# Squares summed in four column tiles, the root moved ahead, and low parts of the first scan's weights moved between normalisation and rotation

## The chip, the cores and the metric

One core of a Trainium2 chip runs the whole program. The time is device microseconds of one execution. A kernel is run several times and the median is given.

## The reference, cut to what matters

A block of three parts runs over `x`, four sequences of 512 tokens with 256 features: half a mixture of experts, a state-space layer with 64 heads, and the same mixture again. Both changed pieces sit in the middle part:

```python
Bm = (x @ WB.T).reshape(B_, L, H, N)          # H = 64 heads, N = 128
Cm = (x @ WC.T).reshape(B_, L, H, N)
Bm = rmsnorm(Bm, Bn_w) + B_bias               # x * rsqrt(mean(x*x) + EPS) * w
Cm = rmsnorm(Cm, Cn_w) + C_bias
theta_cumsum = jnp.cumsum(theta * dt[..., None], axis=1)
Bm = rope(Bm, theta_cumsum)                   # rotation of pairs of features
Cm = rope(Cm, theta_cumsum)
h = at * h + bt * B_prev x_prev + gt * Bt xt  # scan over the tokens of a sequence
yt = einsum('bhn,bhnp->bhp', Ct, h)
```

## The kernel before, in words

**Stages.** A first mixture of experts, then four scans (one for each sequence, numbered 0 to 3), then the second mixture. A short routing stage lies between scans 1 and 2. Scans 0 and 1 also gather rows of the first mixture's result (`gather_turn_pool`, `gather_turn_dve`, L803 on DVE), and scans 2 and 3 scatter rows for the second one.

**A scan.** 64 heads are 32 pairs (`n` counts them through all scans, `q` in one scan). After a preparation (`prep_pe` and the like) the pairs go through a software pipeline. `turn_pe`, `turn_act`, `turn_pool`, `turn_dve` and `turn_sp` each write out a body of four pairs, `j` = 0 to 3, that a hardware loop repeats. The order on each engine is what stands in these functions. Nothing else schedules. In what follows a *turn* is the part of one pair `n`, an *odd* turn one with odd `j`, and a *step* (period) the time from one turn to the next. Engines run freely and wait for each other's semaphores: `e_...` are counted by engines, `a_...` by DMAs.

**What a turn does on each engine**, in this order:

- PE: `ss_pe(n+2)` sums squares (below). `Y_pe(n-2)` (L1391, L1393) makes outputs and waits for DVE's `K_dve2` of the turn before. `G_pe(n-1)` (L1327) multiplies rotated B by rotated C. `tr_pe` (L1336) transposes B. `A_pe(n+3)` (L63, `wb`) projects B and C with a high and a low part of the weights, halves [0, 1] and [2, 3], with `K2_pe` (L1367) between them. `T_pe(n+2)` (L63, `th`) projects the angles.
- ACT: `T_act3` makes cosine and sine, `T_act2` (L1162) rounds the running sum of the angles, `R_act` (L1213, odd turns, needs another function table) takes the root, `K_act` (L1342) copies the transposes out of PSUM, which frees the bank that `A_pe` writes next, and `A_act` (L1206, L1208) copies the projections out and squares them.
- DVE: `T_dve1` (L1148, L1151, waits for `T_pe`), `F_dve2` (L1257, L1262), `T_dve2` (L1157, waits for `T_act2`), `K_dve1` (L1351, waits for `G_pe`), `Y_dve` (odd turns), `F_dve1` (L1251 twice, the normalisation), `R_dve` (L1218, odd turns, the reciprocal of the root), `F_dve3` (L1275 four times, the rotation's products), the gather's L803 in scans 0 and 1, and `K_dve2` (L1376, the states).
- POOL: `D_pool` (L1300), `own_pool` (L1295, waits for `F_dve1`), `F_pool` (L1283, L1284 twice, completes the rotation, waits for `F_dve3`).
- SP issues the DMAs.

**Sums of squares.** `ss_pe` multiplies the squares (`sq4`, [128, 4, 512]: even and odd features of B and of C) by a matrix of ones and zeros. It is four matmuls with 32 result rows each into one PSUM bank: B's in partitions 0 to 31, C's in 32 to 63 (a column tile of PE each), even and odd features added up. The fp32 matmul has two records in the trace. Two turns fill the bank. In the odd turn `R_act` takes the root of 36 rows of 512, `R_sp1` moves eight of them into `rc_in` [128, 32], `R_dve` inverts, `R_sp2` writes them to DRAM and `R_sp3` reads them back copied over all partitions (`rr_bc`), for `F_dve1` of the next turns.

**Scan 0's weights.** Projections use weights split in a high part (fp32 rounded by a copy) and a low part (the difference). Scan 0 makes both and stores them in DRAM (`watt_dram`). Later scans only load them. For each pair in scan 0: SP loads the raw weights (`wb_load_sp` L1023 into `keep`, `th_load_sp` L1031 into `th_raw`), ACT copies (`wb_high_act` L1053, `th_high_act` L1067), DVE subtracts (`wb_low_dve` L1057, `th_low_dve` L1071, both operands in SBUF), and SP stores (L1038, L1043). Raw weights have one buffer, so a load waits for the low part of the pair before, and the high part waits for the load. In the kernel before, the two low parts stand behind rotation and gather:

```python
                F_dve3(e, n, j, q, [1])
                if gathers(b):
                    gather_turn_dve(e, b, n, q, it, j)
                if is_first(b) and not last:
                    wb_low_dve(e, q + 4, j)
                if is_first(b) and not (last and j >= 1):
                    th_low_dve(e, q + 3, j + 1)
                if K:
                    K_dve2(e, p, jp, b * NB + it + (j > 0))
```

## Time and profile before

| | |
|---|---|
| median of 3 runs | 3599.38 us (3589.8 to 3600.61) |
| the profiled execution | 3601.3 us, its span 3599.5 us |
| busy in the span | PE 2897.9 us, DVE 2374.4 us, ACT 1820.9 us, POOL 1539.4 us |
| mean granted clock of TensorE | 0.882 of full speed |
| sums of squares, L1197 | 1024 records, 246.0 us busy |
| low parts, L1057 and L1071 | 32 of each, most of them 2.3 and 1.5 us |
| scans' steady parts, from the span's start | scan 0 700 to 1190 us, scan 1 1360 to 1770, scan 2 1990 to 2400, scan 3 2560 to 2970 |

Busy time is the union of an engine's instructions. Ends of matmuls are modelled, so neighbours overlap by some tenths of a us. Both mixtures and the routing between are not touched by the change. The granted clock is a share of 2.4 GHz.

### The profile page before, as it was taken

What the parts mean: (1) busy time and instruction counts of PE and PEld (TensorE: products, weight loads), DVE (VectorE), ACT (ScalarE), POOL (GpSimd) and SP (SyncE); (2) the same over time, 40 slices, a digit from 0 to 9 for tenths busy, and PEclk for the clock granted to TensorE, in tenths of its full rate; (3) what the DMA queues carried; (4) which work ended last, traced back from release to release, by engine and by line L of the source; (5) the groups of instructions that cost most, each with busy time, mean ns of one, the idle gap of its engine ahead of it and who ended that gap; (6) DMA issues with size and microseconds to landing.
All of it is one profiled execution on the core that took longest, in us unless ns stands there. A gap on an engine that the chain in (4) does not pass through costs nothing.

```text
span 3599.5 us, 84310 instructions
## 1 busy us (share of the span) xinstructions
PE 2897.9 (81%) x28752; PEld 2199.6 (61%) x28752; DVE 2374.4 (66%) x3926; ACT 1820.9 (51%) x3740; POOL 1539.4 (43%) x1420
## 2 busy tenths in 40 slices
PE   5139957788888899999977999999899998279573
PEld 4128846466666657667654667676676676168462
DVE  5214224699999849889945988884888885243135
ACT  1016624566666356666614666663666672046331
POOL 3550050255555416655610555551455553510345
PEclk7559968889899899999978999998999998589785
DMA  9537755466665246556403666642666653467564
GB/s 387 197 123 254 255 163 179 142 183 184 177 184 176 77 139 171 164 162 171 134 3 119 173 172 172 171 134 68 170 172 171 172 160 115 158 206 254 175 205 138
DMA packets 311258, 605.54 MB, mean 168 GB/s; under 512 B 59136, under 2 KB 159616, under 8 KB 310016
## 3 DMA queue, kind: packets, MB, share of 16 engines
q1 hardware_dynamic: 286464, 535.63, 48.9%
q0 software_dynamic: 24576, 67.14, 5.6%
q8 instruction: 120, 1.97, 0.2%
q14 instruction: 98, 0.80, 0.1%
HBM read 446.25 MB, written 155.32 MB: 167 GB/s over the span
## 4 chain that ended last, share of the span: by engine, by line
PE 53%; DVE 19%; issue 10%; another core or an unknown queue 7%; ACT 4%; DMA 4%; POOL 1%; DVEq 1%; SPq 1%; POOLq 0%; ACTq 0%
PE bank L63 15%; PE bank L568 7%; PE bank L1327 4%; DVE tmp L1275 3%; PE bank L1197 3%; PE bank L1393 3%; DVE xbc L1251 3%; DMA rc_in<-decay_t 3%; PE bank L581 2%; PE bank L559 2%; PE bank L1391 2%; PE cs_sn L581 2%; PE bank L1367 2%; DVE rot L1275 2%
## 5 line engine op out<-in xcount | busy, mean ns | idle before, releaser
L63 PE MATMUL bank<-xh,wb 128*128 128x512 f32 x2048 | 685.4, 416 | 73.1 <-ACT btr L1342 43.2
L644 DVE TENSOR_TENSOR hh<-sg,bank 128x96 f32<-128x96 f32 x384 | 97.5, 254 | 596.4 <-ACT sg L619 372.6
L63 PEld LDWEIGHTS bank<-xh,wb 128*128 128x128 f32 x2048 | 373.3, 192 | 190.4 <-ACT btr L1342 63.9
L1206 ACT ACTIVATE xbc<-bank,norm_w 128x512 f32<-128x512 f32 x512 | 350.7, 685 | 240.8 <-PE bank L63 234.1
L1295 POOL TENSOR_TENSOR sq<-cst,rho 128x512 f32<-128x512 f32 x128 | 133.5, 1043 | 742.8 <-DVE xbc L1251 411.3
L1283 POOL TENSOR_TENSOR rot<-rot,tmp 128x512 f32<-128x512 f32 x256 | 341.8, 1335 | 238.3 <-DVE tmp L1275 238.3
L568 PE MATMUL bank<-wgu,xgT 128*128 (+1 forms) x1536 | 343.7, 350 | 107.6 <-issue 68.2
L63 PE MATMUL bank<-xl,wb 128*128 128x512 f32 x1024 | 408.5, 399 | 0.0
L1284 POOL TENSOR_TENSOR rot<-rot,tmp 128x512 f32<-128x512 f32 x256 | 358.7, 1401 | 0.0
L568 PEld LDWEIGHTS bank<-wgu,xgT 128*128 128x128 f32 x1536 | 261.0, 204 | 118.5 <-issue 118.1
L1275 DVE SCALAR_TENSOR_TENSOR rot<-xbc,bias,cs_sn 128x1024 f32<-128x1024 f32 x256 | 325.4, 1271 | 8.4 <-DVE xbc L1251 6.8
L1275 DVE SCALAR_TENSOR_TENSOR tmp<-xbc,bias,cs_sn 128x1024 f32<-128x1024 f32 x256 | 326.2, 1274 | 0.0
L1251 DVE TENSOR_TENSOR xbc<-xbc,rr_bc 128x1024 f32<-128x1024 f32 x256 | 311.7, 1258 | 1.9
L1208 ACT ACTIVATE sq<-bank 128x512 f32<-128x512 f32 x512 | 303.7, 593 | 5.0 <-PE bank L1197 5.0
L1197 PE MATMUL bank<-sq,cst 128*32 128x512 f32 x1024 | 246.0, 601 | 21.7 <-ACT sq L1208 21.7
L1342 ACT ACTIVATE btr<-bank 128x512 f32<-128x512 f32 x256 | 142.0, 594 | 235.4 <-PE bank L1336 235.2
L1393 PE MATMUL bank<-st,rot 128*64 128x16 f32 x3584 | 252.4, 217 | 0.0
L1391 PEld LDWEIGHTS bank<-x1p,sq 128*64 128x64 f32 x2048 | 139.2, 146 | 182.0 <-issue 135.1
L1393 PEld LDWEIGHTS bank<-st,rot 128*64 128x64 f32 x3584 | 239.8, 149 | 0.0
L63 PEld LDWEIGHTS bank<-xl,wb 128*128 128x128 f32 x1024 | 195.9, 191 | 48.6
L574 PE MATMUL cs_sn<-ident,hh 128*96 128x128 f32 x384 | 111.0, 289 | 139.5 <-issue 104.4
L1391 PE MATMUL bank<-x1p,sq 128*64 128x16 f32 x2048 | 150.7, 216 | 80.4 <-DVE st L1376 80.1
(277 smaller groups left out, 6084.7 us busy)
## 6 DMA issues: line engine op xcount, KB each, us to landing
wb<-watt_dram SPq DMA_DIRECT2D x96, 1024.0 KB, 7.7
rr_bc<-rr_dram SPq DMA_DIRECT2D x128, 512.0 KB
yd<-ys SPq DMA_DIRECT2D x96, 512.0 KB
wd<-w_down SPq DMA_DIRECT2D x384, 96.0 KB
watt_dram<-wb SPq DMA_DIRECT2D x32, 1024.0 KB, 5.4
dt_bc<-row_dram SPq DMA_DIRECT2D x256, 128.0 KB
al_bc<-row_dram SPq DMA_DIRECT2D x256, 128.0 KB, 3.2
xd<-xg SPq DMA_DIRECT2D x12, 2048.0 KB, 23.7
```

What stands on the lines that cost most here:

```text
L63: ins = e.matmul(dst, a, m, start=start and c == 0, stop=stop and c == n - 1, skip_group_check=not (start and stop))
L568: ins = e.matmul(gub[n % 2][:, 0:NI2], xgT[n % 2][:, k, :], w, start=k == 0, stop=k == KD - 1)
L581: e.matmul(dnb[n % 2][:, 0:D], hT[n % 2][:, :], wd[n % NWD][:, :], start=True, stop=True).then_inc(e_dn.sem, 1)
L1197: ins = e.matmul(SSB[32 * ty:32 * ty + 32, :], one_hot[:, first:first + 32], sq4[:, 2 * ty + eo, :], start=j % 2 == 0 and eo == 0, stop=j ...
L1206: e.activation(xbc[j % 4][:, i, :], of(i)[:, :], ACT.Copy, scale=norm_w[:, i:i + 1])
L1208: e.activation(sq4[:, i, :], of(i)[:, :], ACT.Square).then_inc(e_X.sem, 1)
L1251: e.tensor_tensor(both, both, r.unsqueeze(1).to_broadcast([P, 2, SEQ]), ALU.mult).then_inc(dst.sem, 1)
L1275: ins = e.scalar_tensor_tensor(o[:, 2 * ty:2 * ty + 2, :], X[:, i, :].unsqueeze(1).to_broadcast([P, 2, SEQ]), bias_of(i), cs_sn[:, :, :], ...
L1283: e.tensor_tensor(R[:, 2 * ty, :], R[:, 2 * ty, :], tmp[:, 2 * ty + 1, :], ALU.subtract)
L1284: ins = e.tensor_tensor(R[:, 2 * ty + 1, :], R[:, 2 * ty + 1, :], tmp[:, 2 * ty, :], ALU.add)
L1391: e.matmul(o, m1[:, (a * TT + t) * CL:(a * TT + t + 1) * CL], c4(x1p[j][:, :])[:, a * TT + t], start=True, stop=True)
L1393: ins = e.matmul(y[CL:P, k, w:w + PW].rearrange("p (a d) -> p a d", a=2), R[:, 2 + eo, CL * k:CL * k + CL], hist[:, eo, :, :, k], start=eo ...
```

## The change

Four things change, the first three in all scans, the last in scan 0 alone.

1. `ss_pe` works on halves of 256 tokens: eight matmuls instead of four, each of 256 columns instead of 512, at partitions 0, 32, 64 and 96 (four column tiles). The result lies in 100 rows of 256. `R_act` takes the root of that, into a buffer of its own (`stdr`, [100, 256]) instead of rows of `decay_t`. `R_sp1` and `R_sp2` each issue two DMAs instead of one.
2. On ACT, `R_act` stands ahead of `T_act2` instead of behind it.
3. On SP, `R_sp1` stands ahead of the transfers of `dt_bc`, `end_bc`, `th` and `wb` instead of behind them.
4. In scan 0, DVE's low parts stand between normalisation (with `R_dve`) and rotation. The angle weights' parts are made in the turn that uses them instead of the turn before. ACT's high parts stand ahead of `K_act` instead of near the end of the turn. SP loads raw angle weights at the end of its turn.

```diff
--- before.py
+++ after.py
@@ -184,8 +184,9 @@
         neg_a = sb("neg_a", [NH, 1])
         bias = sb("bias", [P, NP, 4])
         norm_w = sb("norm_w", [P, 4])
-        stdr = decay_t[0:36, :, :, :].rearrange("p k q a -> p (k q a)")
-        NORM_ROWS = slice(28, 36)
+        HALF = SEQ // 2
+        stdr = sb("stdr", [100, HALF])[:, :]
+        NORM_ROWS = [slice(28, 36), slice(92, 100)]
         rc_in, rc = sb("rc_in", [P, 32]), sb("rc", [P, 32])
 
         dks = [xc[:, i, :] for i in range(2)]
@@ -1192,10 +1193,12 @@
                 e.wait_ge(e_sr.sem, e_sr.at(m // 2 if isinstance(m, int) else m >> 1))
             e.wait_ge(e_X.sem, e_X.at(4 * (m + 1)))
             for eo in range(2):
-                for ty in range(2):
-                    first = 30 - 28 * (1 - ty) - 2 * (j % 2)
-                    ins = e.matmul(SSB[32 * ty:32 * ty + 32, :], one_hot[:, first:first + 32], sq4[:, 2 * ty + eo, :],
-                                   start=j % 2 == 0 and eo == 0, stop=j % 2 == 1 and eo == 1, skip_group_check=True)
+                for half in range(2):
+                    for ty in range(2):
+                        first = 30 - 28 * (1 - ty) - 2 * (j % 2)
+                        g = 64 * half + 32 * ty
+                        ins = e.matmul(SSB[g:g + 32, 0:HALF], one_hot[:, first:first + 32], sq4[:, 2 * ty + eo, half * HALF:(half + 1) * HALF],
+                                       start=j % 2 == 0 and eo == 0, stop=j % 2 == 1 and eo == 1, skip_group_check=True)
             ins.then_inc(e_ssm.sem, 1)
 
         def A_act(e, m, j, parts=range(4), of=by_turns):
@@ -1209,12 +1212,12 @@
 
         def R_act(e, gm):
             e.wait_ge(e_ssm.sem, e_ssm.at(2 * (gm + 1)))
-            e.wait_ge(a_r1.sem, a_r1.at(gm))
-            e.activation(stdr, SSB[0:36, :], ACT.Sqrt, scale=1.0 / NS, bias=eps_nm[0:36, 0:1]).then_inc(e_sr.sem, 1)
+            e.wait_ge(a_r1.sem, a_r1.at(2 * gm))
+            e.activation(stdr, SSB[0:100, 0:HALF], ACT.Sqrt, scale=1.0 / NS, bias=eps_nm[0:100, 0:1]).then_inc(e_sr.sem, 1)
 
         def R_dve(e, gm):
-            e.wait_ge(a_r1.sem, a_r1.at(gm + 1))
-            e.wait_ge(a_r2.sem, a_r2.at(gm))
+            e.wait_ge(a_r1.sem, a_r1.at(2 * (gm + 1)))
+            e.wait_ge(a_r2.sem, a_r2.at(2 * gm))
             e.reciprocal(rc[:, :], rc_in[:, :]).then_inc(e_rc.sem, 1)
 
         e_rc = ev("e_rc")
@@ -1224,15 +1227,18 @@
             e.nop(nofuse=True)
             e.wait_ge(e_rc.sem, e_rc.at(gm))
             e.nop(nofuse=True)
-            e.dma_start(rc_in[:, :], stdr[NORM_ROWS, :].rearrange("r (c w) -> r c w", w=32)).then_inc(a_r1.sem, 16)
+            for h in range(2):
+                e.dma_start(rc_in[CL * h:CL * h + CL, :], stdr[NORM_ROWS[h], :].rearrange("r (c w) -> r c w", w=32)).then_inc(a_r1.sem, 16)
 
         def R_sp2(e, gm, par):
             e.wait_ge(e_rc.sem, e_rc.at(gm + 1))
             e.nop(nofuse=True)
-            e.dma_start(rr_dram[par].rearrange("r (c w) -> (r c) w", w=32), rc[:, :]).then_inc(a_r2.sem, 16)
+            for h in range(2):
+                dst = rr_dram[par][:, h * HALF:(h + 1) * HALF].rearrange("r (c w) -> r c w", w=32)
+                e.dma_start(dst, rc[CL * h:CL * h + CL, :]).then_inc(a_r2.sem, 16)
 
         def R_sp3(e, gm, par):
-            e.wait_ge(a_r2.sem, a_r2.at(gm + 1))
+            e.wait_ge(a_r2.sem, a_r2.at(2 * (gm + 1)))
             e.nop(nofuse=True)
             e.wait_ge(e_xcc.sem, e_xcc.at(2 * (gm - 1)))
             e.nop(nofuse=True)
@@ -1467,10 +1473,14 @@
                     stage_act(e, b, n, q, it, j)
                 if not (first and j == 0):
                     T_act3(e, n, j)
+                if RG:
+                    R_act(e, gm + 1)
                 if T:
                     T_act2(e, n + 1, j + 1)
-                if RG:
-                    R_act(e, gm + 1)
+                if is_first(b) and not last:
+                    wb_high_act(e, q + 4, j, it * 2 + j // 2 + 2)
+                if is_first(b) and not (last and j >= 2):
+                    th_high_act(e, q + 2, j, it * 2 + j // 2 + 1)
                 if K:
                     K_act(e, p, jp, 0, 0)
                 if last and j >= 2:
@@ -1485,10 +1495,6 @@
                     A_act(e, n + 3, j + 3, [1], behind_transposes)
                 if RG:
                     e.activation(std[:, 0:1], half_pi[:, 0:1], ACT.Sin)
-                if is_first(b) and not last:
-                    wb_high_act(e, q + 4, j, it * 2 + j // 2 + 2)
-                if is_first(b) and not (last and j >= 1):
-                    th_high_act(e, q + 3, j + 1, it * 2 + (j + 1) // 2 + 1)
                 if A:
                     A_act(e, n + 3, j + 3, [2, 3], behind_transposes)
 
@@ -1530,14 +1536,14 @@
                 F_dve1(e, n, j, b * NB + it + 1)
                 if RG:
                     R_dve(e, gm + 1)
+                if is_first(b) and not last:
+                    wb_low_dve(e, q + 4, j)
+                if is_first(b) and not (last and j >= 2):
+                    th_low_dve(e, q + 2, j)
                 F_dve3(e, n, j, q, [0])
                 F_dve3(e, n, j, q, [1])
                 if gathers(b):
                     gather_turn_dve(e, b, n, q, it, j)
-                if is_first(b) and not last:
-                    wb_low_dve(e, q + 4, j)
-                if is_first(b) and not (last and j >= 1):
-                    th_low_dve(e, q + 3, j + 1)
                 if K:
                     K_dve2(e, p, jp, b * NB + it + (j > 0))
 
@@ -1552,8 +1558,10 @@
                     wb_store_sp(e, q + 3, j + 1)
                 if is_first(b) and not last:
                     wb_load_sp(e, b, q + 4, j)
-                if is_first(b) and not (last and j >= 2):
-                    th_store_sp(e, q + 2, j)
+                if is_first(b) and not (first and j == 0) and not (last and j == 3):
+                    th_store_sp(e, q + 1, j + 1)
+                if RG:
+                    R_sp1(e, gm + 1)
                 if not (last and j >= 2):
                     e.wait_ge(e_tu.sem, e_tu.at(n + 1))
                     e.nop(nofuse=True)
@@ -1561,7 +1569,7 @@
                     e.wait_ge(e_H.sem, e_H.at(n - 1))
                     e.nop(nofuse=True)
                     end_sp(e, q + 2, j + 2)
-                if not (last and j >= 1):
+                if not is_first(b) and not (last and j >= 1):
                     e.wait_ge(e_th.sem, e_th.at(n + 2))
                     e.nop(nofuse=True)
                     th_load_sp(e, b, q + 3, j + 1)
@@ -1570,8 +1578,6 @@
                     e.nop(nofuse=True)
                     if not is_first(b):
                         wb_load_sp(e, b, q + 4, j)
-                if RG:
-                    R_sp1(e, gm + 1)
                 if not (last and j >= 2):
                     e.wait_ge(e_D.sem, e_D.at(n + 1))
                     e.nop(nofuse=True)
@@ -1579,6 +1585,8 @@
                 if RG:
                     R_sp2(e, gm + 1, (j // 2 + 1) % 2)
                     R_sp3(e, gm + 1, (j // 2 + 1) % 2)
+                if is_first(b) and not (last and j >= 1):
+                    th_load_sp(e, b, q + 3, j + 1)
 
         def pairs_pe(e, b):
             N, NB, G = b * NP, NP // UN, b * (NP // 2)
@@ -1606,7 +1614,6 @@
             A_act(e, N + 2, 2, [0, 1])
             T_act3(e, N, 0)
             if is_first(b):
-                th_high_act(e, 2, 0, 1)
                 wb_high_act(e, 3, 1, 1)
             A_act(e, N + 2, 2, [2, 3])
             e.wait_ge(e_x12.sem, e_x12.at(b + 1))
@@ -1637,8 +1644,6 @@
             N, NB, G = b * NP, NP // UN, b * (NP // 2)
             T_dve1(e, N, 0, G + 1)
             T_dve2(e, N, 0)
-            if is_first(b):
-                th_low_dve(e, 2, 0)
             if is_first(b):
                 wb_low_dve(e, 3, 1)
             turn_dve(e, b, 0, True, False)
```

In the lists below, line numbers are those of each kernel: most of the changed kernel's are 1 to 10 higher. First DVE, an odd turn of scan 0, before:

```order
L1251 TENSOR_TENSOR xbc<-xbc,rr_bc 128x1024 x2
L1218 RECIPROCAL rc<-rc_in 128x32
L1275 SCALAR_TENSOR_TENSOR rot<-xbc,bias,cs_sn 128x1024
L1275 SCALAR_TENSOR_TENSOR tmp<-xbc,bias,cs_sn 128x1024
L1275 SCALAR_TENSOR_TENSOR rot<-xbc,bias,cs_sn 128x1024
L1275 SCALAR_TENSOR_TENSOR tmp<-xbc,bias,cs_sn 128x1024
L803 SCALAR_TENSOR_TENSOR keep<-ykq,w,keep 128x256
L1057 TENSOR_TENSOR wb<-keep,wb 128x1024
L1071 TENSOR_TENSOR th<-th_raw,th 128x256
L1376 SCALAR_TENSOR_TENSOR st<-end_bc,bank 64x128 x2
```

and the same turn in the changed kernel:

```order
L1257 TENSOR_TENSOR xbc<-xbc,rr_bc 128x1024 x2
L1221 RECIPROCAL rc<-rc_in 128x32
L1058 TENSOR_TENSOR wb<-keep,wb 128x1024
L1072 TENSOR_TENSOR th<-th_raw,th 128x256
L1281 SCALAR_TENSOR_TENSOR rot<-xbc,bias,cs_sn 128x1024
L1281 SCALAR_TENSOR_TENSOR tmp<-xbc,bias,cs_sn 128x1024
L1281 SCALAR_TENSOR_TENSOR rot<-xbc,bias,cs_sn 128x1024
L1281 SCALAR_TENSOR_TENSOR tmp<-xbc,bias,cs_sn 128x1024
L804 SCALAR_TENSOR_TENSOR keep<-ykq,w,keep 128x256
L1382 SCALAR_TENSOR_TENSOR st<-end_bc,bank 64x128 x2
```

The two low parts moved from behind the gather to behind the reciprocal.

ACT, the start of an odd turn of scan 0, before (the high parts came near the turn's end):

```order
L1170 ACTIVATE cs_sn<-ths,half_pi 128x512
L1162 ACTIVATE bank<-cum,magic 128x512
L1213 ACT_TABLE_LOAD
L1213 ACTIVATE decay_t<-bank,eps_nm 36x512
L1342 ACTIVATE btr<-bank 128x512 x2
...
L1487 ACT_TABLE_LOAD
L1487 ACTIVATE std<-half_pi 128x1
L1053 ACTIVATE wb<-keep 128x1024
L1067 ACTIVATE th<-th_raw 128x256
```

and now:

```order
L1171 ACTIVATE cs_sn<-ths,half_pi 128x512
L1216 ACT_TABLE_LOAD
L1216 ACTIVATE stdr<-bank,eps_nm 100x256
L1163 ACTIVATE bank<-cum,magic 128x512
L1054 ACTIVATE wb<-keep 128x1024
L1068 ACTIVATE th<-th_raw 128x256
L1348 ACTIVATE btr<-bank 128x512 x2
```

Root and table load are ahead of the rounding, and the high parts are ahead of the copies of the transposes.

SP, an odd turn of scan 0 in the changed kernel, from its second DMA on:

```order
L1024 DMA keep<-w_att 128x1024
L1044 DMA watt_dram<-th 256x1x256
L1231 DMA rc_in<-stdr 64x1x32 x2
L1127 DMA dt_bc<-row_dram 64x512 x2
L1127 DMA end_bc<-row_dram 64x128 x2
L1127 DMA al_bc<-row_dram 64x512 x2
L1238 DMA rr_dram<-rc 8x8x32 x2
L1247 DMA rr_bc<-rr_dram 64x4x512 x2
L1032 DMA th_raw<-w_att 128x256
```

`rc_in` was one DMA between `end_bc` and `al_bc`, and `th_raw` stood ahead of it. Now `th_raw` is the last of the turn, behind `rr_bc`.

## Rows read from the trace of the kernel before

**Rows 1.** Busy time by stage, scans 0, 1, 2: PE, PEld, DVE, ACT, POOL; clock, DMA share, GB/s.

```profile
700.00:1190.00 490.00, 429.51 (x5068) 322.16 (x5069) 473.23 (x545) 310.20 (x550) 267.20 (x218) 0.91 0.62 181
1360.00:1770.00 410.00, 388.97 (x4960) 286.68 (x4960) 366.42 (x476) 268.41 (x476) 239.11 (x211) 0.99 0.58 165
1990.00:2400.00 410.00, 390.79 (x5064) 287.33 (x5063) 364.31 (x464) 284.21 (x518) 237.89 (x219) 1.00 0.60 170
```

**Rows 2.** Line L1218, once in two turns: ns min/median/max, first to last start (scans 0 to 2).

```profile
L1218 DVE RECIPROCAL rc<-rc_in x14: 345/348/353, 705.8 to 1171.2; 128x32 f32<-128x32 f32 x14
L1218 DVE RECIPROCAL rc<-rc_in x13: 345/352/354, 1379.8 to 1753.1; 128x32 f32<-128x32 f32 x13
L1218 DVE RECIPROCAL rc<-rc_in x14: 343/352/354, 1991.4 to 2382.3; 128x32 f32<-128x32 f32 x14
```

**Rows 3.** Waits, 1360 to 1770 us (scan 1): us in total, times, longest.

```profile
DVE sq L1351 <- PE bank L1327: 15.7, 26, 1.0
DVE bank L1148 <- PE bank L63: 10.8, 12, 2.1
DVE rc L1218 <- DMA rc_in<-decay_t: 8.9, 9, 1.2
```

**Rows 4.** Waits, 1990 to 2400 us (scan 2).

```profile
DVE sq L1351 <- PE bank L1327: 14.1, 27, 1.0
PE bank L63 <- ACT btr L1342: 13.0, 27, 1.1
DVE rc L1218 <- DMA rc_in<-decay_t: 12.7, 12, 1.8
DVE bank L1148 <- PE bank L63: 10.7, 13, 1.2
```

**Rows 5.** Timeline, one `ss_pe` of scan 2: start, us, engine, instructions merged.

```profile
2206.43 1.91 PE L1197 MATMUL bank<-sq,cst 128*32 128x512 f32 x8
2206.43 0.14 PEld L1197 LDWEIGHTS bank<-sq,cst 128*32 128x32 f32 x4 [0.37 <-ACT sq L1208]
2206.89 0.12 PEld L1197 LDWEIGHTS bank<-sq,cst 128*32 128x32 f32 x2 [0.31 <-issue]
2207.32 0.12 PEld L1197 LDWEIGHTS bank<-sq,cst 128*32 128x32 f32 x2 [0.31 <-issue]
```

**Rows 6.** Timeline of scan 0: DVE around the low parts, and POOL there.

```profile
961.12 2.29 DVE L1057 TENSOR_TENSOR wb<-keep,wb 128x1024 fp32r<-128x1024 f32 x1
963.32 1.48 DVE L1071 TENSOR_TENSOR th<-th_raw,th 128x256 fp32r<-128x256 f32 x1
964.73 0.84 DVE L1376 TENSOR_TENSOR_SCAN st<-end_bc,bank 64x128 f32<-64x128 f32 x2
...
960.85 1.47 POOL L1283 TENSOR_TENSOR rot<-rot,tmp 128x512 f32<-128x512 f32 x1
962.28 2.25 POOL L1284 TENSOR_TENSOR rot<-rot,tmp 128x512 f32<-128x512 f32 x1
...
973.25 1.04 POOL L1295 TENSOR_TENSOR sq<-cst,rho 128x512 f32<-128x512 f32 x1 [2.69 <-DVE xbc L1251]
```

**Rows 7.** Lines L1057 and L1071, all of scan 0, ns min/median/max.

```profile
L1057 DVE TENSOR_TENSOR wb<-keep,wb x32: 1215/2295/2317, 613.1 to 1176.8; 128x1024 fp32r<-128x1024 f32 x32
L1071 DVE TENSOR_TENSOR th<-th_raw,th x32: 418/1485/1503, 614.3 to 1193.7; 128x256 fp32r<-128x256 f32 x32
```

**Rows 8.** Timeline of scan 0: SP's issue of a raw load, ACT's rounding and high part; then DMA's median us to landing.

```profile
946.09 0.41 SPq L1023 DMA_DIRECT2D keep<-w_att  x1
...
949.20 0.69 ACT L1162 ACTIVATE bank<-cum,magic 128x512 f32<-128x512 f32 x1 [3.71 <-DVE cum L1151]
...
958.62 1.05 ACT L1053 ACTIVATE wb<-keep 128x1024 fp32r<-128x1024 f32 x1
...
keep<-w_att SPq DMA_DIRECT2D x32, 512.0 KB, 6.0
```

**Rows 9.** Timeline of scan 2's preparation on ACT: the root behind `ss_pe`.

```profile
1951.90 1.28 ACT L1213 ACT_TABLE_LOAD   x1 [3.54 <-PE bank L1197]
```

## The prediction

> **What bounds the kernel now.** The page's busy times name PE (81% of the span), but a share of the whole says little here, so I first read busy time stage by stage. In scan 0 DVE is busy 473 of 490 us and PE 430 [rows 1]: DVE is the bound. In scans 1 and 2 PE is busy 389 and 391 of 410 us, DVE 366 and 364: PE is the bound and DVE follows closely. The change touches the four scans only.
>
> The next view is the start of one instruction that comes once in two turns, L1218 [rows 2]. It gives the step per turn: scan 0 (1171.2 - 705.8) / 13 / 2 = 17.9 us, scan 1 (1753.1 - 1379.8) / 12 / 2 = 15.55, scan 2 (2382.3 - 1991.4) / 13 / 2 = 15.03. Scan 3 runs the same body as scan 2, and I take scan 2's step for it.
>
> The third view is the waits. They tell what stands second in line, which decides how much of a saving is kept. In scan 1 (410 / 15.55 = 26.4 turns) DVE waits 15.7 us for `G_pe`, 10.8 for `T_pe` and 8.9 for `rc_in`: 1.34 us a turn [rows 3]. Without any wait DVE would need 15.55 - 1.34 = 14.2 us a turn. In scan 2 (27.3 turns) the same three are 14.1, 10.7 and 12.7 us, 1.37 a turn, so DVE's floor is 13.66 [rows 4]. PE waits there 13.0 us, 0.48 a turn, for ACT's copy of the transposes.
>
> **Squares in four column tiles.** One `ss_pe` takes 1.91 us [rows 5]. Its eight records do not run one after another: four weight loads start at 2206.43 (for the first two slots), two at 2206.89 and two at 2207.32. So a slot is 0.44 us and holds two records. Four slots of 0.44 and an end of 0.15 give 1.91. The two column tiles already run side by side, with different moving data. The changed form has 16 records of half the columns. If four run side by side, there are again four slots, each of 0.22: 4 x 0.22 + 0.15 = 1.03 us. That saves **0.88 us a turn**. Four loads must fit into a slot: at the start four loads take 0.14 us together [rows 5], less than 0.22.
>
> No row shows four column tiles of 32 at once, so the bounds are: no gain (two at a time, eight slots of 0.22) and 0.88. I take 0.88, since the pair in the rows loses nothing against its own slots.
>
> The rows show the loads of 2206.89 inside the 1.91 us, beside a running pair. The Trainium skill ("TensorE: Matmul & The Clock Gate", Part 3) says that weight loads overlap running matmuls only where the row group differs, which column tiles of full height never do: by that rule loads stand outside the slots (rival d), and the trace does not agree with it for two tiles. For three column tiles the same page states a speedup of 2.38, not 3; by that, an estimate of the saving would be 0.65 us a turn.
>
> In scans 2 and 3 PE is the bound, so the step falls from 15.03 to about 14.15. DVE's floor is 13.66, and a part of the waits behind it stays, since DVE and PE hand work to each other twice in a turn. I take 14.2, a saving of 0.85. Not all 32 turns run steadily; I count 30 a scan. 60 x 0.85 = **51 us**. In scan 1 the step falls from 15.55 to 14.67, above DVE's floor of 14.2, and I take the same 0.85: 30 x 0.85 = **25 us**. The bounds of this term: below, half of it, if DVE's alternation of short and long turns becomes the bound; above, DVE's floors themselves, 1.37 x 60 + 1.34 x 30 = 122 us instead of 76. In scan 0 PE is not the bound, and this part is worth nothing.
>
> **The root first, on ACT and on SP.** In odd turns `R_act` starts before the rounding. It removes no work. DVE's wait for `rc_in` (0.47 us a turn in scan 2 [rows 4]) goes, but DVE waits in these scans only because PE is late, so by itself this gives nothing; it pays by lowering the floor that part one runs into, and is counted there. The price is on the same engine. The table load starts only when `ss_pe` is done [rows 9], takes 1.28 us, and the rounding now stands behind it, with `T_dve2` behind that. In the best case this is hidden (`ss_pe` ends before the turn's `T_act3` does) and costs nothing; in the worst the whole load shows, 1.28 us in each odd turn, 0.64 a turn. DVE's floor in scans 2 and 3 would then be 13.66 + 0.64 = 14.3 instead of the 14.2 I take, 6 us in 60 turns. I take nothing, since a shorter `ss_pe` also ends earlier. The two extra DMA issues at `R_sp1` and `R_sp2` add about 1 us to SP in odd turns, and its transfers of `dt`, `end`, `th` and `wb` wait for the root. They are for the next turn or later, 14 us away; I cost them at nothing.
>
> **Low parts in scan 0.** Alone, in the preparation, the two take 1.215 and 0.418 us. Inside a turn almost all take 2.3 and 1.49 [rows 7]. The timeline says why [rows 6]. The first starts at 961.12 while POOL's L1283 runs until 962.32, and ends 1.1 us after that, at 963.41. POOL's L1284 starts at 962.28, takes 2.25 us, and ends 1.1 us after the low part did. The second low part starts at 963.32 and ends 0.27 us after POOL's 964.53. So one engine at a time has what both need. From 961.12 to 964.73 DVE spends 3.61 us on work that takes about 1.14 + 0.34 = 1.48 us alone.
>
> In the new place POOL has one instruction, L1295, 1.04 us [rows 6], which starts when the normalisation ends, just when the low parts do. Whichever goes first, DVE passes it once: 1.48 + 0.96 = 2.44 us. The saving is 3.61 - 2.44 = **1.17 us a turn**, 30 x 1.17 = **35 us**. Bounds: 0 if POOL's work meets DVE elsewhere instead, and 2.13 a turn, 64 us, if L1295 gets out of the way.
>
> The same rule is in the Trainium skill ("SBUF — State Buffer", on the port pair shared by VectorE and GpSimd): two SBUF inputs on VectorE against a GpSimd read block each other fully. The trace agrees, as far as [rows 6] show. By that rule the rotation's products, which read one operand from PSUM, do not meet POOL at all, and the bound of 0 would drop out.
>
> What lies beside: PE in scan 0 needs 429.5 / 490 x 17.9 = 15.7 us a turn, less 0.88, so 14.8 against the new step of 16.7 [rows 1]. The high part's copy (1.05 us for `wb` [rows 8], a fourth of the columns for `th`) now stands in front of ACT's `K_act` and delays `A_pe` by up to 1.4 us. PE's 1.9 us of slack covers it, and costs it if gone. The raw load must also come sooner. Now it is issued at 946.09, lands 6.0 us later at 952.1, and is used at 958.62. In the changed order it is needed right behind the rounding, which ends at 949.89, less the 1.2 us by which the turn gets shorter: 948.7 [rows 8]. But it also starts sooner, since the low part it waits for has four products (L1275) and the gather behind it instead of ahead, some 5 us: 941 + 6.0 = 947. About 1.7 us are left.
>
> **The sum.** 51 + 25 + 35 = 111 us against the profiled execution's own 3601.3 us: 3490. The median of the runs lies 1.9 us below that execution. I predict **3488 us**.
>
> **Rivals.**
>
> (a) *Two tiles at a time.* The new form gives eight slots of half the length, no gain; only scan 0 gains. 3601 - 35 = 3566 us. For it: no row shows four. Against it: nothing in the rows makes two special. Chance 0.10.
>
> (b) *Scan 0 gains nothing.* The raw load is late, ACT waits for it in front of `K_act`, and PE behind ACT. If it lands 5 us later than above, 1.7 and PE's remaining slack are used up and the 1.17 us go too: 3488 + 35 = 3523 us. Scans 1 to 3 are as forecast. Chance 0.10.
>
> (c) *Slower.* The 16 records run one at a time, because a load and a matmul of another tile shut each other out. `ss_pe` would take 16 x 0.22 + 0.15 = 3.7 us, 1.8 more. In scans 1 to 3 that is 90 x 1.8 = 162 us on the bound; in scan 0 PE would need 17.5 us, more than the 16.7, so 35 shrinks to 12. 3601 - 12 + 162 = 3751 us. It decides from the point where the records start less than 1.6 at a time: then the loss passes scan 0's 35 us. The pairs in [rows 5] speak against it. Chance 0.03.
>
> (d) *Loads outside the slots.* Four tiles run together, but each slot first waits for its four loads, 0.14 us [rows 5]: 0.56 a turn of the 0.88 is lost, 0.32 stays. 3601 - 90 x 0.32 - 35 = 3537 us. For it: a slot of 0.22 leaves loads half the time they had. Chance 0.05.
>
> **How the numbers follow.** My forecast has 0.72, with its own range of 3455 (DVE near its floors) to 3525 (half of PE's saving, scan 0 as taken). To leave out no more than 2 in 10, the range goes from 3455 to 3545; it holds (b) and (d) and leaves out (a), (c) and some 0.05 of worse mixtures. About 0.3%, 11 us, is what a measurement of this kernel can tell from no change. Faster than that: all but (c) and worse mixtures, 0.95. Within: 0.02. Slower: (c) and a little, 0.03.
>
> **What would show it.** The 16 records of a `ss_pe` in about 1.0 us, loads four at a time (right), in 1.9 (a) or over 3 (c). Steps per turn from the reciprocal's starts: 16.7, 14.7, 14.2, 14.2. DVE busy 95% or more in scans 2 and 3, and no wait for `rc_in`. In scan 0 low parts that take 2.2 + 0.3 or 1.2 + 1.3 us, and POOL's L1284 at 1.3 us throughout. Wrong: ACT waiting for the raw load, DVE's `T_dve2` waiting for ACT's rounding, or a lower granted clock in scans 1 to 3 than 0.99.

## The result, and the profile after

The changed kernel takes 3693.69 us (median of 4 runs, 3682.48 to 3701.94) against 3594.59 for the kernel before, a ratio of 1.027 (95% interval 1.024 to 1.031). The forecast was 3488 us and faster. The profiled execution of the changed kernel took 3687.81 us.

Busy time by stage, a stretch of scans 0, 1 and 2 each (columns as in [rows 1]):

```profile
740.00:1170.00 430.00, 361.66 (x4504) 287.58 (x4504) 371.97 (x465) 261.21 (x465) 224.05 (x187) 0.84 0.58 177
1385.00:1780.00 395.00, 352.34 (x4671) 278.72 (x4671) 333.74 (x439) 243.45 (x434) 219.67 (x194) 0.93 0.55 158
2050.00:2430.00 380.00, 336.86 (x4624) 265.83 (x4626) 315.80 (x403) 246.84 (x454) 206.05 (x192) 0.94 0.55 162
```

PE is busy 89% in scans 1 and 2, where it was 95% [rows 1], and its granted clock is 0.93 and 0.94 where it was 0.99 and 1.00: part of each scan runs at 1.2 GHz. DVE is busy less in scan 0, as meant. No engine is nearer to full than before, so something between the engines must be late. The starts of the reciprocal, once in two turns, are to be set beside [rows 2]:

```profile
L1221 DVE RECIPROCAL rc<-rc_in x14: 343/345/347, 703.4 to 1180.9; 128x32 f32<-128x32 f32 x14
L1221 DVE RECIPROCAL rc<-rc_in x12: 343/343/346, 1389.5 to 1750.0; 128x32 f32<-128x32 f32 x12
L1221 DVE RECIPROCAL rc<-rc_in x12: 339/346/347, 2019.2 to 2371.3; 128x32 f32<-128x32 f32 x12
```

The steps are 18.4, 16.4 and 16.0 us a turn, where the forecast had 16.7, 14.7 and 14.2 and the kernel before has 17.9, 15.6 and 15.0. Scan 3 is slower too (16.2 against 15.1).

The two local effects came as forecast. One `ss_pe` of scan 2 (timeline, as [rows 5]), and the low parts of scan 0 with POOL beside them (as [rows 6]):

```profile
2200.70 1.07 PE L1200 MATMUL bank<-sq,cst 128*32 128x256 f32 x16
2200.70 0.59 PEld L1200 LDWEIGHTS bank<-sq,cst 128*32 128x32 f32 x16 [0.37 <-ACT sq L1211]
...
962.12 1.16 DVE L1058 TENSOR_TENSOR wb<-keep,wb 128x1024 fp32r<-128x1024 f32 x1
963.20 1.26 DVE L1072 TENSOR_TENSOR th<-th_raw,th 128x256 fp32r<-128x256 f32 x1
964.38 1.27 DVE L1281 SCALAR_TENSOR_TENSOR rot<-xbc,bias,cs_sn 128x1024 f32<-128x1024 f32 x1
...
962.24 1.94 POOL L1301 TENSOR_TENSOR sq<-cst,rho 128x512 f32<-128x512 f32 x1 [4.00 <-DVE xbc L1257]
```

The squares take 1.07 us instead of 1.91, with all sixteen loads inside them: four column tiles run together. From the first low part to the rotation DVE spends 964.38 - 962.12 = 2.26 us instead of 3.61. L1301 takes 1.94 us here and 1.04 in [rows 6]: it ends 0.9 us after the first low part, so the two pass one after the other. The Trainium skill ("SBUF — State Buffer", "Who interferes with whom") says that a VectorE instruction with two SBUF inputs contends with a GpSimd instruction that reads SBUF. The trace agrees, by the same 1.94 us against 1.04.

The loss is in the waits. Those of scan 2 (1990 to 2400 us, beside [rows 4]):

```profile
DVE xbc L1257 <- DMA rr_bc<-rr_dram: 42.1, 12, 5.6
PE bank L1397 <- DVE st L1382: 24.7, 12, 4.5
...
SPq L1227 <- ACT stdr L1216: 133.4, 13, 11.8
SPq L1242 <- DMA rr_dram<-rc: 47.3, 12, 4.4
```

DVE's normalisation waits for the broadcast of the reciprocals, a wait that [rows 4] don't have. SP issues its transfers in the order of the program. It stands 133 us at `R_sp1` for the root, and then 3.9 us each time for the small write of the reciprocals to land. The chain of waits from SP's hold-up to DVE (start, us, what):

```profile
2236.41 0.70 SPq L1231
...
2241.15 0.60 SPq L1034
...
2242.09 0.58 SPq L1026
...
2244.19 1.44 SPq L1238
...
2245.68 4.76 DMA rr_dram<-rc
...
2250.65 0.64 SPq L1247
...
2251.33 7.42 DMA rr_bc<-rr_dram
...
2259.92 1.23 DVE xbc L1257
```

Read it downwards. The root's transfer, then `dt`, `end`, `th` (L1034) and the 1 MB of `wb` (L1026) all go out in one burst, since they stood behind the root. The small write (L1238) is issued 2.1 us after the `wb` load and takes 4.8 us to land; only then may its broadcast go, 7.4 us more.

In scan 0 the waits (700 to 1200 us) are others:

```profile
ACT wb L1054 <- DMA keep<-w_att: 61.9, 13, 7.9
PE bank L63 <- ACT btr L1348: 47.2, 27, 6.0
DVE bank L1149 <- PE bank L63: 32.9, 13, 3.7
```

ACT waits for the raw load in front of its copies of the transposes, PE waits for the copies, DVE for PE.

### The profile page after: what moved, and what is told of

It is laid out like the page before. It is cut to its first block, busy times and chain, and to the rows that moved or that the text cites. A ratio compares the mean times of both kernels' runs of the same rounds, so it can differ in the third digit from the quotient of the medians.

```text
span 3686.0 us, 86397 instructions
## 1 busy us (share of the span) xinstructions
PE 2877.2 (78%) x29776; PEld 2280.2 (62%) x29776; DVE 2327.2 (63%) x3926; ACT 1810.0 (49%) x3740; POOL 1531.5 (42%) x1420
## 4 chain that ended last, share of the span: by engine, by line
PE 33%; DMA 17%; issue 13%; DVE 12%; SPq 11%; ACT 6%; another core or an unknown queue 6%; POOL 2%; DVEq 0%; ACTq 0%; POOLq 0%
DMA rr_bc<-rr_dram 7%; PE bank L569 7%; PE bank L63 7%; DMA rr_dram<-rc 5%; SPq L1127 4%; DMA keep<-w_att 3%; DVE tmp L1281 3%; PE bank L560 2%; PE cs_sn L582 2%; DVE xbc L1257 2%; PE bank L582 2%; SPq L1231 2%; DVE rot L1281 1%; PE bank L1333 1%
## 5 line engine op out<-in xcount | busy, mean ns | idle before, releaser
L63 PE MATMUL bank<-xh,wb 128*128 128x512 f32 x2048 | 706.0, 427 | 113.6 <-ACT btr L1348 77.9
L63 PEld LDWEIGHTS bank<-xh,wb 128*128 128x128 f32 x2048 | 386.7, 199 | 231.6 <-ACT btr L1348 97.6
L1301 POOL TENSOR_TENSOR sq<-cst,rho 128x512 f32<-128x512 f32 x128 | 151.2, 1181 | 876.3 <-DVE xbc L1257 556.1
L1289 POOL TENSOR_TENSOR rot<-rot,tmp 128x512 f32<-128x512 f32 x256 | 340.7, 1331 | 246.3 <-DVE tmp L1281 246.3
L63 PE MATMUL bank<-xl,wb 128*128 128x512 f32 x1024 | 417.8, 408 | 0.0
L1257 DVE TENSOR_TENSOR xbc<-xbc,rr_bc 128x1024 f32<-128x1024 f32 x256 | 307.7, 1243 | 147.9 <-DMA rr_bc<-rr_dram 146.0
L1290 POOL TENSOR_TENSOR rot<-rot,tmp 128x512 f32<-128x512 f32 x256 | 330.2, 1290 | 0.0
L1397 PE MATMUL bank<-x1p,sq 128*64 128x16 f32 x2048 | 159.5, 221 | 156.4 <-DVE st L1382 156.0
L1397 PEld LDWEIGHTS bank<-x1p,sq 128*64 128x64 f32 x2048 | 147.6, 154 | 211.7 <-DVE st L1382 122.9
L1399 PE MATMUL bank<-st,rot 128*64 128x16 f32 x3584 | 272.0, 223 | 3.7 <-issue 3.7
L1399 PEld LDWEIGHTS bank<-st,rot 128*64 128x64 f32 x3584 | 259.0, 158 | 3.8 <-issue 3.8
L1333 PE MATMUL bank<-rot 64*64 64x64 f32 x8192 | 208.0, 259 | 30.3 <-POOL rot L1290 20.8
```

Source lines behind the costliest of these rows:

```text
L63: ins = e.matmul(dst, a, m, start=start and c == 0, stop=stop and c == n - 1, skip_group_check=not (start and stop))
L1257: e.tensor_tensor(both, both, r.unsqueeze(1).to_broadcast([P, 2, SEQ]), ALU.mult).then_inc(dst.sem, 1)
L1289: e.tensor_tensor(R[:, 2 * ty, :], R[:, 2 * ty, :], tmp[:, 2 * ty + 1, :], ALU.subtract)
L1290: ins = e.tensor_tensor(R[:, 2 * ty + 1, :], R[:, 2 * ty + 1, :], tmp[:, 2 * ty, :], ALU.add)
L1301: e.tensor_tensor(blocks(own), constant("diag_mask").unsqueeze(1).to_broadcast([P, 2 * TT, CL]), r.unsqueeze(2).to_broadcast([P, 2 * TT, C ...
L1333: ins = e.matmul(o, R[h, eo, CL * k:CL * k + CL], R[h, 2 + eo, CL * k:CL * k + CL], start=eo == 0, stop=eo == 1)
```

## Experiments

The kernel before takes 3595 to 3599 us in some series of runs (that of the result, and two experiments below) and 3344 to 3354 us in the others. These are called the *first chip* and the *second chip* below. The names stand for the two levels of time: the record has several chip numbers for the second, and one of them (8) for both. About 231 of the 250 us lie before the first reciprocal of scan 0 and behind the fifteenth of scan 3. The steps are nearly the same: 17.9, 15.2, 15.0, 14.9 on the second, 17.9, 15.6, 15.1, 15.1 on the first. Ratios are always to the kernel before in the same series. A step is the mean over 24 turns, from the third to the fifteenth reciprocal of a scan. All ran on the second chip unless said otherwise.

A step from one profile has its own scatter. The fastest version below, profiled twice, has 14.8 and 15.1 us in scan 2. Differences in a step under 0.3 us are no evidence.

**The kernel before on the second chip.**

> The kernel before, for its profile on the chip of the experiments, where its median was 3349 us. Theory one (the square kernel's freed TensorE time turns into idle time and then into stretches at the lower of the clock's two levels): in scan 2 this profile shows the granted clock at 1.00, no L1327 or L1336 group of a turn that takes 2 us, and a step per turn of 15.1 to 15.2 us, the same as with the squares in four tiles (15.13). Theory two (this chip itself has such stretches, whatever the kernel): the clock is 0.93 to 0.97 here too, and the steps of the squares' kernel can be compared with these as they stand.

Measured: 3349.9 us (one run), clock 0.915, steps as above; clock 1.00 in scans 1 and 2 and 0.99 in scan 3. This is theory one. In its SP timeline the write follows the `wb` load by 8.6 us, and SP waits for it 11.9 us in 11 turns (1990 to 2400 us):

```profile
2102.95 0.57 SPq L1025 DMA_DIRECT2D wb<-watt_dram  x1
2105.31 0.71 SPq L1227 DMA_DIRECT2D rc_in<-decay_t  x1
2111.59 0.32 SPq L1232 DMA_DIRECT2D rr_dram<-rc  x1
2113.19 1.29 SPq L1241 DMA_DIRECT2D rr_bc<-rr_dram  x2
...
SPq L1236 <- DMA rr_dram<-rc: 11.9, 11, 2.0
```

**The changed kernel with root's transfers put back.**

```
 turn_sp:  -  if RG: R_sp1(...)      (ahead of the wait for e_tu)
           +  if RG: R_sp1(...)      (behind the wb load, ahead of the wait for e_D)
```

> The changed kernel with R_sp1 back behind the loads of dt, end, th and wb on SP (all scans); all else as changed. Theory A (order on SP: the root's issue holds the 1 MB load of wb back until just ahead of the small write of rc, which then waits behind it in the queue): steps of scans 1 to 3 fall from about 16.1 to 14.2 to 14.6 us, the write of rc lands within 2 us, DVE's wait for rr_bc goes, total 3510 to 3550 us; scan 0 stays near 18.4 us a turn. Theory B (the doubled small DMAs, more issues and more packets' latency): DVE still waits for rr_bc, total over 3640 us.

Measured: 1.000 (0.998 to 1.003); steps 18.3, 15.4, 14.7, 14.9. DVE's wait for `rr_bc` is gone (0.9 us from 1850 to 2450 us). The changed kernel has 1.025 to 1.027 on the first chip, and this one has 1.000 on the second, so the slowdown goes with this one line. The comparison crosses the chips, since the changed kernel was not run on the second. The next experiment stays on the second chip. Theory A is right on the wait and wrong on the time: the forecast gain does not come.

**Only root's transfers first,** the kernel before with `R_sp1` ahead of the wait for `e_tu`:

> The kernel before with R_sp1 moved ahead of dt, end, th and wb on SP and nothing else. Theory A: the write of rc lands after 4 to 5 us instead of 1.5, DVE waits for rr_bc, steps of scans 1 to 3 rise by 0.5 to 1.3 us: total 3640 to 3720 us. Theory B: there is no doubled DMA, so no difference, 3595 us.

Measured: 1.049 (1.046 to 1.051), and in a second series, again on the second chip, 1.050 (1.047 to 1.052); steps 17.8, 17.2, 16.9, 16.9. It is theory A's mechanism, at more than its price (0.5 to 1.3 us a turn expected, about 1.9 measured). Scan 0, which has no `wb` load from `watt_dram`, loses nothing. The write's time to landing from 1850 to 2450 us, for the kernel before (there on this chip) and then for this one, with this one's chain of waits in scan 2:

```profile
DMA to landing us min/median/max: 1.4/1.4/3.8
```

```profile
DMA to landing us min/median/max: 2.3/6.0/7.7
...
2053.62 0.56 SPq L1025
...
2055.70 5.32 DMA rr_dram<-rc
2061.21 0.63 SPq L1241
2061.89 6.77 DMA rr_bc<-rr_dram
...
2077.66 1.23 DVE cum L1151
...
2079.62 1.28 ACT L1213
2080.92 0.69 ACT decay_t L1213
2081.72 0.69 SPq L1227
```

It is a closed loop: broadcast, DVE down to the next prefix sum, root, SP's burst, write, broadcast. Two turns take 33.7 us on average.

**Is it the `wb` load that holds the write?** The changed kernel, in odd turns of scans 1 to 3 with that load behind `R_sp3`:

```
 -  if not is_first(b): wb_load_sp(e, b, q + 4, j)
 +  if not is_first(b) and not RG: wb_load_sp(e, b, q + 4, j)
 ...
    R_sp3(...)
 +  if RG and not last and not is_first(b): wb_load_sp(e, b, q + 4, j)
```

> The changed kernel with the root's transfers still first, but in odd turns of scans 1 to 3 the 1 MB load of wb moved behind R_sp3. Theory A: the small write of rc no longer stands behind 1 MB, lands in 1.5 to 2.5 us instead of 4.7, and the wait for rr_bc falls from 3.5 us in two turns to under 1: total 3520 to 3570 us, unless wb itself comes late (then PE waits for it and the step is over 15). Theory B: no change, 3690 us.

Measured: 1.073 (1.071 to 1.076). Steps of scans 1 to 3: 17.7, 17.7, 17.5. SP's wait for the write fell to that of the kernel before, and PE now waits for the load itself (1990 to 2400 us):

```profile
SPq L1242 <- DMA rr_dram<-rc: 11.9, 11, 1.3
...
PE bank L63 <- DMA wb<-watt_dram: 69.2, 12, 7.6
```

So the load does hold the write, and it has no 5 us to give: "for the next turn or later" was wrong for it too. DVE's wait for `rr_bc` falls from 146.0 us in the whole execution to 65.8 and does not go, though the write lands quickly. What is left may be the length of SP's burst itself; no run separates it.

**The root early on both engines,** and **the changed kernel again** (on the first chip):

> e4 with the root ahead of the rounding on ScalarE as well, squares and scan 0 as before. Steps of scans 1 to 3 so far: 15.2 to 15.0 before, 17.2 to 16.9 with the transfers first, 16.4 to 16.0 in the changed kernel. Theory one (the early root lets SP go on sooner, and that is why the changed kernel pays only half): steps 15.9 to 16.4, the wait for rr_bc 130 to 160 us in place of 206, ratio 1.022 to 1.035. Theory two (the squares, which bring the sum 0.84 us sooner, are the other half): steps 16.5 to 16.8, ratio over 1.035.

> The changed kernel itself on the chip of the experiments, to have its parts and their sum beside one another: squares alone 1.005, root's transfers first alone 1.049, all but the transfers 1.000. Theory one (transfers first is what makes it slower, and its cost is about that of e4 less what the other parts give): 1.035 to 1.055. Theory two (on the first chip it was 1.027, and the earlier root on ScalarE gives back part of the cost, since SP is held up for less time): 1.020 to 1.035.

Measured: 1.021 (1.019 to 1.024), steps 17.9, 15.9, 15.8, 15.9, wait for `rr_bc` 147.5 us; and 1.025 (1.022 to 1.028), steps 18.1, 16.4, 16.0, 16.0, wait 136.6 us. The first is theory one, with steps and ratio at the lower edge of its ranges. The second falls in theory two's range, but on the first chip. The early root frees SP sooner: its wait for the root falls from 656.3 us in the whole execution (transfers first alone) to 493.6, and the price from 4.9% to 2.1%, both on the second chip. SP's wait for the write to land is nearly the same in both (232.8 and 223.8 us). So the held write is one part of the loop's length, and the time at which the root comes is another. The squares are not needed for the lower price: without them it is no higher.

**Only the squares.** The kernel before with four column tiles and the transfers that they need:

> The kernel before with the squares in four column tiles and the doubled DMAs alone; orders on ACT and SP and scan 0's low parts as before. Theory A: each ss_pe 1.07 instead of 1.91 us, steps of scans 1 to 3 near 14.7, 14.3, 14.3, scan 0 17.9: total 3520 to 3545 us. Theory B: DVE waits longer for rc_in (one more issue of 0.7 us) or for rr_bc, total 3580 us or more.

Measured: 1.005 (1.003 to 1.007); steps 18.3, 15.5, 15.1, 15.1; clock 0.888. Theory A's gain is not there, and DVE's wait for `rc_in` is longer, as in theory B (76.9 us against 64.2). Stages of 24 turns in scan 2, the kernel before on this chip and then this one:

```profile
1900.30:2260.60 360.30, 346.07 (x4503) 255.39 (x4503) 323.78 (x409) 253.97 (x461) 213.91 (x193) 1.00 0.61 172
```

```profile
1922.30:2285.30 363.00, 336.78 (x4668) 266.52 (x4665) 322.00 (x408) 248.77 (x458) 211.44 (x193) 0.95 0.59 171
```

24 x 0.84 = 20 us of PE's work are gone, but PE is busy only 9 us less, since it runs part of the time at the lower clock (a matmul of L1342 takes 273 ns there at the median and up to 477). Its idle time grows from 14 to 26 us, and the step has not fallen. DVE is busy 323.8 and 322.0 us, 13.5 and 13.4 a turn. The waits in the same two stretches:

```profile
DVE rc L1218 <- DMA rc_in<-decay_t: 15.2, 9, 2.5
DVE sq L1351 <- PE bank L1327: 8.2, 15, 0.7
```

```profile
DVE rc L1221 <- DMA rc_in<-stdr: 20.7, 12, 2.8
PE bank L1397 <- DVE st L1382: 19.5, 12, 2.7
DVE bank L1149 <- PE bank L63: 10.1, 8, 1.9
```

DVE's wait for `G_pe` falls from 8.2 to 1.6 us, but those for `rc_in` and for `T_pe` (3.2 before) grow: together 26.6 us before, 32.4 now. PE waits 19.5 us for DVE's states where it waited 6.4.

**Only the two transfers,** `rc_in` and `rr_dram` in two halves each, squares as before:

> Before with one edit: rc_in and rr_dram are each moved by two transfers of half the rows in place of one; squares in two tiles as before. Theory one (the squares in four tiles gain a little and their second transfers take it back; with both the ratio was 1.005): this one reads 1.004 to 1.010, with the reciprocal's wait for rc_in up by 8 to 15 us on 64 us. Theory two (the transfers cost nothing, and it is TensorE's clock or the order around it that takes the 0.84 us back): ratio 0.999 to 1.002.

Measured: 1.002 (1.001 to 1.004), clock 0.915, wait for `rc_in` 74.0 us against 64.2. It lies between the theories: by the medians it explains about half of the 0.5%, and it does not explain the clock.

**Squares with idle products,** eight more per two turns behind the sum, and eight per turn ahead of it:

```
 ss_pe:  +  for the four tiles g, twice:
         +      e.matmul(SSB[g:g + 32, HALF:SEQ], before[:, 0:32], every..., start=True, stop=True)
```

> The squares' kernel with eight idle products of the same form behind the sum's signal in every other turn, whose result nobody reads: TensorE has 1.1 us more work per two turns, off the path of the sum. Theory one (the freed time becomes idle time, and then a stretch at the lower clock level): less idle ahead of the y products, fewer half-clock stretches, granted clock up from 0.93 to 0.96 in scan 2, and the time is no worse than the squares alone, 3345 to 3370 us (ratio 0.998 to 1.005). Theory two (TensorE is simply the bound, and its work per turn sets the step): the step grows by 0.5 us a turn and the ratio is 1.010 or more. Theory three (the half-clock stretches come from elsewhere): clock unchanged at 0.93 with the step 0 to 0.5 us longer.

> The squares' kernel with eight idle products of the same form ahead of each turn's sum, into the half of the bank that the sum leaves free (the sums of squares come out other with them): TensorE is busy again for as long as in before, and the sum is as late, while layout and transfers are those of the squares' kernel. So far: squares alone 1.0051, granted clock 0.888 (before 0.915); the two transfers alone 1.0023, clock 0.915. Theory one (0.84 us less work leaves TensorE idle before the y products, and the clock falls): the clock is back at 0.91 or more, scan 0's step back from 18.31 to 17.9 to 18.1 us, ratio 1.000 to 1.004, so more work on TensorE makes the kernel no slower or even faster than the squares alone. Theory two (the clock falls for another reason, such as 16 small records with their weight loads in place of 8): clock 0.885 to 0.895 and ratio 1.010 or more.

Both kernels compute wrong sums of squares, so they are of use for their times alone. Measured: 1.011 (1.009 to 1.014), clock 0.906, steps 18.1, 16.1, 15.2, 15.2; and 1.014 (1.012 to 1.016), clock 0.913, steps 19.0, 15.6, 15.1, 15.0. No theory holds whole: the clock came back as theory one had it, the ratio is theory two's. In scans 2 and 3 the padded kernel has the clock back:

```profile
1934.20:2296.50 362.30, 347.94 (x5077) 269.93 (x5077) 323.37 (x409) 251.10 (x461) 215.81 (x193) 0.99 0.60 171
```

and the same step as the squares at 0.95. So there the lower clock goes with idle time, and is not what holds the step. Where these two kernels are slow, the instruction transfers (queue q8) pile up, here from 630 to 1065 us, in scan 0, for the kernel before and for the padded one (packets, MB, share):

```profile
q8 instruction: 6, 0.10, 0.1%
```

```profile
q8 instruction: 49, 0.80, 0.8%
```

Pair by pair, in the padded kernel's scan 0 the five pairs of 39 to 42 us have 5 or 6 such transfers, the others, of 35.0 to 36.5 us, 3 or 4. The others are as short as before's (35 to 36.5) and shorter than those of the squares alone (36 to 38): in scan 0 the clock does seem to count. That the loads cause the long pairs is argued from this coincidence; no run took them away.

**Root ahead on ACT,** with the squares:

> Before with the squares in four tiles and the root ahead of the rounding on ScalarE; transfers and scan 0 as before. Theory one (SP issues the root's transfers only behind those of the turn, so an earlier root changes nothing, and the rounding comes 0.6 to 1 us later, in odd turns): 3350 to 3385 us, ratio 1.000 to 1.011, like the squares alone (1.005). Theory two (the reciprocal's wait for rc_in, 21.5 us in 13 turns of scan 2 with the squares alone, was the root's late start): that wait falls under 8 us and the ratio to 0.99 to 0.997.

Measured: 1.009 (1.007 to 1.012), wait for `rc_in` 68.7 us against 76.9, and a new wait of DVE for the rounding of 18.4 us. No gain, as theory one has it. In scans 1 to 3 this kernel is the same program as the changed kernel with root's transfers put back (1.000), yet its steps there are 15.7, 15.1, 15.1 against 15.4, 14.7, 14.9. Why is open. So a ratio of 1.005 or 1.009 is measured for a kernel, but that all of it belongs to the squares or to the root is not shown.

**Scan 0 by itself.** The kernel before with the new place of low parts, high parts and raw loads:

> Before with nothing but the new place of the low parts, the high parts and the raw loads of scan 0; squares, root and the rounding as before, root's transfers where they were. Theory one (what the low parts gain on VectorE is given back because the raw load is issued late and ScalarE's high part, now ahead of the copies, waits for it): ACT waits for the raw load over 3 us in every other turn, VectorE's low parts take 2.3 to 2.5 us together, scan 0's step stays at 17.9 to 18.4 us, and the ratio is 0.997 to 1.008. Theory two (the prediction's: the low parts' 1.2 us per turn is kept, and what spoiled scan 0 in the changed kernel were the root's transfers alone): step 16.9, ratio 0.990.

Measured: 0.999 (0.997 to 1.000). DVE is busy 386.7 us in 24 turns instead of 417.2, 1.27 us less a turn, and the step is 17.9 as before. This is theory one. PE waits for ACT's copies and ACT for the raw load:

```profile
PE bank L63 <- ACT btr L1342: 54.5, 24, 5.7
ACT wb L1053 <- DMA keep<-w_att: 36.3, 12, 5.2
```

Then the same kernel with the high parts behind the copies:

```
 turn_act:  -  wb_high_act(...); th_high_act(...)   (behind T_act2)
               K_act(e, p, jp, 1, ...)
            +  wb_high_act(...); th_high_act(...)
```

> The kernel e5 (before with nothing but the new places in scan 0) with the two high parts behind K_act's second copy on ScalarE again. In e5's scan 0 TensorE waited 54.5 us in 24 turns for L1342's copies (9.5 us on before), which stood behind a high part that waited 36.3 us for its raw load. Theory one (the gain of the low parts is given back there): the wait of L63 for L1342 falls under 20 us, the raw load has 1.5 to 2 us more time, scan 0's step falls from 17.86 to 17.0 to 17.5 us, ratio 0.992 to 0.997. Theory two (the low parts, now ahead of the rotation, wait for the high part instead, and VectorE with everything behind it stops): the wait of L1057 for L1053 goes over 1.5 us a turn and the ratio is 1.000 or more.

Measured: 0.988 (0.986 to 0.990), step of scan 0 16.4 us: theory one, with a gain beyond its range. The same two waits (620 to 1050 us):

```profile
PE bank L63 <- ACT btr L1342: 15.0, 20, 1.3
ACT wb L1053 <- DMA keep<-w_att: 3.3, 3, 2.4
```

And with the raw load earlier on SP as well (in scan 0, `R_sp3` and the theta load behind the next turn's raw load):

> e10, and in scan 0 SP issues the raw load of the next turn directly behind R_sp2 or the alpha rows, ahead of R_sp3, the theta load and the store. Theory one (it is the late raw load that keeps scan 0 from using VectorE's 1.2 us per turn): raw load issued 2 to 3 us earlier in every other turn, ScalarE's wait for it under 10 us in scan 0, step 16.7 to 17.3 us, ratio 0.988 to 0.994, and under e10. Theory two (scan 0's step is held by TensorE's or by the transfers' chain, VectorE's time is not what bounds it): step 17.7 or more and ratio 0.997 or more, with the saved time as a wait of VectorE for TensorE's bank.

> e11 once more, the fastest version so far. Theory one (its gain lies in scan 0 alone, whose step is the same on both chips): 40 to 50 us faster than before on either chip, ratio 0.986 to 0.989 where before takes 3600 us. Theory two (it depends on the chip's clock): under 30 us.

Measured: 0.986 (0.985 to 0.988) at 3298 us, and 0.985 (0.983 to 0.987); step 16.4 in both. It is the fastest version, 46 us under the kernel before, though no more than level with the one above: the raw load was no longer late. The kernel before took 3348.7 us in the second series too, so its two theories, which are about a chip where it takes 3600, stay open.

**All parts but transfers first, on the good scan 0,** and **root ahead on it** (first chip):

> The changed kernel with root's transfers back behind those of the turn, and scan 0 arranged as in e11. It has e1's squares and root order (1.0004) with e11's scan 0. Theory one (the parts are independent): ratio is that of e1 less what e11 has gained on e5, 0.990 to 0.997. Theory two (in scan 0, where VectorE has now slack, TensorE's 0.84 us can be kept as well, since it is now the bound): scan 0's step is under e11's by 0.3 to 0.8 us and the ratio 0.982 to 0.989.

> e11 (scan 0's low parts ahead of the rotation, raw load early, squares and transfers as before) and the root ahead of the rounding on ScalarE; SP's order unchanged. e11's reciprocal still waits 59.7 us for rc_in, in a chain that runs from VectorE's prefix sum over the rounding and the root. Theory one (that wait is part of what holds scans 1 to 3 at 14.8 to 15.2 us): the wait falls to 50 us or less and the ratio by 0.001 to 0.004 below e11's 0.986. Theory two (SP issues the transfer only behind wb's load, so the root's 0.7 us change nothing, while the rounding is 2 us later in odd turns): ratio 0.986 to 0.991, wait 55 to 60 us.

Measured: 0.991 (0.989 to 0.992), steps of scans 0 and 1 16.8 and 15.5 against 16.4 and 15.2: squares, split transfers and early root together cost 0.4% here. And 0.989 (0.986 to 0.991), with the wait for `rc_in` down to 39.4 us in the whole execution from the 50.3 of the kernel before. Steps of scans 1 to 3 are 15.7, 15.2, 15.1 against 15.6, 15.1, 15.1. The step has not followed. Another wait came up that the kernel before does not have, for the rounding that now stands behind the root:

```profile
DVE nfr L1157 <- ACT bank L1162: 41.2, 47, 0.9
```

## Why the prediction was wrong

**The failing step is the sentence on `R_sp1`:** "its transfers of `dt`, `end`, `th` and `wb` wait for the root. They are for the next turn or later, 14 us away; I cost them at nothing." Alone this place on SP costs 4.9% (about 160 us), and 2.1% with the early root; with it put back the changed kernel is level with the kernel before. Two things were missed. I priced the transfers by when their data is used and not by what they are queued ahead of: the reciprocals' small write, on which everything of the next two turns depends, now follows the 1 MB load by 2.1 us and not by 8.6, and lands after 5 to 6 us and not 1.4. And SP waits for the root 133 us in scan 2, a wait to which I gave no length, so everything behind it comes in one burst between the root and the write.

**"PE is the bound", so "the step falls from 15.03 to about 14.15", failed too.** The size of the squares' saving was right (0.84 us measured, 0.88 forecast). Sixteen records in 1.07 us with all loads inside refute rivals (a), (c) and (d). But the kept gain was nothing instead of 0.85 a turn (at most 0.3, in one scan of one profile). A busy share of 95% was taken for a bound. DVE's floor of 13.66 was worked out by taking away its waits for PE and for `rc_in`. When PE got faster they did not shrink (26.6 us, then 32.4 in 24 turns), and PE idled for DVE. That they are part of loops through PE, ACT and two transfers is how I read this. The padded kernel shows best that PE's work does not set the step: eight more matmuls a turn and a clock of 0.99, the same step in scans 2 and 3. What does set it was not found. The early root also had a price that I put at nothing, "since a shorter `ss_pe` also ends earlier": with the shorter `ss_pe` it took 8 us off DVE's wait for `rc_in` in the whole execution and brought 18 us of waiting for the rounding (root ahead on ACT); on the good scan 0, without the squares, it was 11 us off and 41 us on.

**Scan 0.** The low parts' saving was forecast at 1.17 us, measured 1.27 of DVE's busy time. The failing step is "PE's 1.9 us of slack covers it": the high parts in front of `K_act` cost PE up to 6 us in a turn, since they wait for the raw load. The step was 17.9 us instead of 16.7 even with root's transfers where they were. So rival (b) came true in its mechanism, at a probability of 0.10. "About 1.7 us are left" was wrong: right behind the low parts shown above, the raw load was issued at 968.69, behind two other waits of SP and 5.4 us after the low part that frees its buffer had ended (963.28), where I had put its start by the data alone. With the high parts behind the copies the step falls by 1.5 us, even more than the 1.2 I had claimed: in scan 0 "DVE is the bound" was right.

**The lower clock** in scans 1 to 3 was named as a sign of error, and it came. In these runs it goes with PE's idle time: 0.91 to 0.93 with transfers first alone (PE idle some 8 to 10% of these scans), 0.94 to 0.96 with the squares alone (7 to 8%), 0.99 with the padding (4 to 5%).

## What to carry to other kernels

When a wait moves forward on an in-order queue, list the transfers behind it and what comes after *them* on the same path: here a late 1 MB load bunched up with the next small transfer of a dependent chain and held it for 4 to 5 us. An engine that is 95% busy need not be the bound: its neighbours' waits must shrink with its work. Where they hand work back and forth through transfers, try the engine's part by itself first, for instance by adding work of the same length and looking whether the step grows. A saving on the engine that is the bound (here DVE in scan 0) is kept only if the feeding step is put where its late case blocks nobody.
